# Row gathers, norm terms and row 0 in the passage from the embedding to the attention

## The reference

```python
# embedding: LoRA (rank 16) on a table of 32000 rows, with a norm over the whole table
base = weight[x]
result = base + (lora_A.T[x] @ lora_B.T) * 2.0
direction = weight + lora_A.T @ lora_B.T * 2.0
direction_norm = sqrt(sum(direction * direction, axis=0))          # one number for each of 512 columns
h = result * magnitude * direction_norm
# attention: 16 heads of 32, ternary weights, activations quantized by row
h = h + attn(layernorm(h))
# feed-forward: shared expert, and 2 of 8 routed experts of width 352
h = h + ffn(layernorm(h))
```

## Time and profile before

| what | value |
|---|---|
| median of 3 runs | 1496.45 us (1494.9 to 1499.45) |
| the profiled execution, own time | 1491.15 us |
| its span, first to last instruction | 1489.4 us |
| PE busy | 1387.3 us, 93% |
| DVE busy | 1115.1 us, 75% |
| ACT busy | 876.0 us, 59% |
| POOL busy | 410.3 us, 28% |
| mean granted TensorE clock | 0.983 |

### The profile page before, as it was taken

One profiled execution on the slowest core, in us unless ns is written; L12 is line 12 of the kernel. 1 busy time (PEld: TensorE's weight loads), 2 busy tenths in 40 slices (PEclk: granted clock), 3 DMA queues, 4 the chain that ended last, 5 costly groups with the idle time before them and its releaser, 6 DMA issues.

```text
span 1489.4 us, 37546 instructions
## 1 busy us (share of the span) xinstructions
PE 1387.3 (93%) x14294; PEld 1135.9 (76%) x14294; DVE 1115.1 (75%) x2210; ACT 876.0 (59%) x1506; POOL 410.3 (28%) x503
## 2 busy tenths in 40 slices
PE   6587869999999998999999999999999999999998
PEld 1121137777777776999999999988989889999997
DVE  4477847999989986686558787878778777677776
ACT  4688946777778885333335656666566665433331
POOL 6500054445445432013111211111111110034333
PEclk9899979999999999999999999999999999999999
DMA  9999952322322211121116778777776776434366
GB/s 343 385 384 363 418 154 47 79 65 73 75 64 73 69 58 69 61 103 51 48 30 194 252 264 272 237 257 250 256 270 233 249 255 226 176 129 152 129 211 213
DMA packets 77907, 269.43 MB, mean 181 GB/s; under 512 B 9696, under 2 KB 10336, under 8 KB 71392
## 3 DMA queue, kind: packets, MB, share of 16 engines
q1 hardware_dynamic: 61360, 223.88, 42.1%
q0 software_dynamic: 16432, 44.05, 11.3%
HBM read 224.12 MB, written 43.78 MB: 180 GB/s over the span
## 4 chain that ended last, share of the span: by engine, by line
PE 27%; DVE 12%; issue 9%; ACT 8%; DMA 3%; another core or an unknown queue 0%; DVEq 0%; ACTq 0%; SPq 0%
PE up_ps L536 4%; PE up_ps L537 4%; PE up_ps L538 4%; DVE w_split L1693 4%; ACT w_split L1611 4%; DMA w_stage<-packed 3%; PE down_ps L537 3%; PE down_ps L538 3%; PE down_ps L536 3%; DVE h L1835 2%; ACT h_hi L1634 1%; DVE w_split L1694 1%; PE S L536 1%; PE S L537 1%; PE S L538 1%
## 5 line engine op out<-in xcount | busy, mean ns | idle before, releaser
L536 PE MATMUL up_ps<-xT_hi,w_split 128*128 128x256 f32 x1008 | 289.3, 287 | 12.0 <-DVE h L1854 9.8
L538 PE MATMUL up_ps<-xT_hi,w_split 128*128 128x256 f32 x1008 | 285.7, 283 | 0.0
L537 PE MATMUL up_ps<-xT_lo,w_split 128*128 128x256 f32 x1008 | 285.7, 283 | 0.0
L1634 ACT ACTIVATE h_hi<-h 128x256 fp32r<-128x256 f32 (+1 forms) x192 | 80.3, 418 | 267.0 <-DVE h L1835 203.9
L536 PEld LDWEIGHTS up_ps<-xT_hi,w_split 128*128 128x128 f32 x1008 | 193.4, 192 | 16.3 <-issue 13.7
L537 PEld LDWEIGHTS up_ps<-xT_lo,w_split 128*128 128x128 f32 x1008 | 193.6, 192 | 1.2
L538 PEld LDWEIGHTS up_ps<-xT_hi,w_split 128*128 128x128 f32 x1008 | 193.6, 192 | 0.0
L1579 POOL DMA_INDIRECT xr<-x_rows,slot_tokens x71 | 77.0, 1084 | 422.3 <-PE S L1998 377.8
L1611 ACT ACTIVATE w_split<-w_stage 128x1408 fp32r<-128x1408 f32 (+1 forms) x120 | 165.6, 1410 | 24.7 <-DMA w_stage<-packed 23.0
L536 PE MATMUL down_ps<-w_split,h_hi 128*128 128x512 f32 (+1 forms) x405 | 159.7, 394 | 3.1 <-DVE H L1813 3.1
L538 PE MATMUL down_ps<-w_split,h_lo 128*128 128x512 f32 (+1 forms) x405 | 160.9, 397 | 0.0
(11 more groups left out here) (320 smaller groups left out, 3384.2 us busy)
## 6 DMA issues: line engine op xcount, KB each, us to landing
W<-table SPq DMA_DIRECT2D x48, 1280.0 KB, 9.1
w_stage<-packed SPq DMA_DIRECT2D x80, 704.0 KB
w_stage<-packed SPq DMA_DIRECT2D x40, 768.0 KB, 4.4
slot_rows<-y_rows SPq DMA_DIRECT2D x32, 512.0 KB
xr<-x_turned SPq DMA_DIRECT2D x31, 512.0 KB
x_rows<-x SPq DMA_DIRECT2D x32, 256.0 KB, 2.0
x_turned<-x2T SPq DMA_DIRECT2D x32, 256.0 KB, 3.9
out<-H SPq DMA_DIRECT2D x32, 256.0 KB
```

The source lines that it names most:

```text
L536: pe.matmul(out, a_hi, b_hi, start=first, stop=False)
L537: pe.matmul(out, a_hi, b_lo, start=False, stop=False)
L538: return pe.matmul(out, a_lo, b_hi, start=False, stop=last)
L1634: act.activation(h_hi[odd][0:f, j, :], h[0:f, j, :], ACT.Copy).then_inc(h_hi_done, 1)
```

## The change

In `embed`: `EARLY_ROWS` is 5 instead of 6, and POOL waits for the last tile of the table before it issues them. ACT's copy of `sums_ps` and the tiles `square_sums` and `share` are gone. DVE adds the two tiles of `acc`, adds `product`, and adds `sums_ps` times 1/32; PE sums only that one tile. PE makes products that nobody reads (`keep_busy`): two behind the sum, one behind the spread.

In `attend`: PE begins with six more such products, and its waits for the router's weights move to their first use. DVE multiplies row 0 with `S_bc` in place of POOL, and makes its constants behind row 0's statistics. POOL multiplies rows 1 and 2 late in its step instead of first. DVE takes the statistics of rows 1 and 2 behind the scales of the row before, and `QT` of row 0 behind those. PE makes V of row 0 behind its Q and K.

In `experts`: the down products wait for all three parts of their low weights.

```diff
-EARLY_ROWS = 6
+EARLY_ROWS = 5
...
-            pool.wait_ge(w_in[SLOTS - 1], 16 * TRIPS)
+            arrived, before = tile_in[-1]
+            pool.wait_ge(arrived, before + 16)
             for i in range(EARLY_ROWS):
                 early_row(i)
...
-            act.wait_ge(summed, BY_TILE + (CHUNKS - BY_TILE) * (CHUNK_TILES - len(ADDED_TILES)))
-            act.activation(square_sums[:, :], sums_ps[:, :], ACT.Copy).then_inc(sums_out, 1)
...
+            tiles_added = FOLDED + (CHUNKS - BY_TILE) * len(ADDED_TILES)
+            dve.wait_ge(added, tiles_added)
+            dve.tensor_tensor(acc[:, 0, :], acc[:, 0, :], acc[:, 1, :], ALU.add).then_inc(added, 1)
             dve.wait_ge(crossed, done(CHUNKS - 1))
             dve.scalar_tensor_tensor(out=product[:, :], in0=cross_ps[:, :], scalar=2.0 * LORA_SCALE, in1=b_rep[:, :],
-                                     op0=ALU.mult, op1=ALU.mult).then_inc(terms_made, 1)
+                                     op0=ALU.mult, op1=ALU.mult).then_inc(added, 1)
+            dve.wait_ge(added, tiles_added + 2)
+            dve.tensor_tensor(acc[:, 0, :], acc[:, 0, :], product[:, :], ALU.add).then_inc(added, 1)
+            dve.wait_ge(added, tiles_added + 3)
+            dve.wait_ge(summed, BY_TILE + (CHUNKS - BY_TILE) * (CHUNK_TILES - len(ADDED_TILES)))
+            dve.scalar_tensor_tensor(out=acc[:, 0, :], in0=sums_ps[:, :], scalar=1.0 / DH, in1=acc[:, 0, :],
+                                     op0=ALU.mult, op1=ALU.add).then_inc(terms_made, 1)
...
+            def keep_busy(times):
+                for _ in range(times):
+                    pe.matmul(sums_ps[:, :], ones[:, :], b_rep[:, :], start=True, stop=True)
...
-            pe.wait_ge(added, FOLDED + (CHUNKS - BY_TILE) * len(ADDED_TILES))
-            for i in range(len(ADDED_TILES)):
-                add_up(acc[:, i, :], ones[:, 0:1], False, False)
             pe.wait_ge(terms_made, PRODUCT)
-            add_up(product, ones[:, 0:1], False, False)
-            pe.wait_ge(sums_out, 1)
-            add_up(square_sums, share[:, :], False, True).then_inc(totalled, 1)
+            add_up(acc[:, 0, :], ones[:, 0:1], False, True).then_inc(totalled, 1)
+            keep_busy(2)
...
             mm.then_inc(spread, 1)
+            keep_busy(1)
```

The attention's POOL, DVE and PE, and the experts' PE:

```diff
+            def scale_row(seq):
+                pool.wait_ge(h_in[seq.i % ROW_SLOTS], 16 * (seq.i // ROW_SLOTS + 1))
+                pool.tensor_tensor(row(H, seq.i), row(H, seq.i), S_bc[:, :], ALU.mult).then_inc(rows_scaled, 1)
+                pool.wait_ge(rows_scaled, seq.next)
...
-                if ahead3.yes:
-                    pool.wait_ge(h_in[ahead3.i % ROW_SLOTS], 16 * (ahead3.i // ROW_SLOTS + 1))
...
+                if ahead3.yes and ahead3.i > 2:
+                    scale_row(ahead3)
...
                 if ahead3.yes:
+                    if 0 < ahead3.i <= 2:
+                        scale_row(ahead3)
                     if EARLY_ROWS <= ahead3.i + ROWS_AHEAD < SEQS:
...
+            dve.wait_ge(h_in[0], 16)
+            dve.tensor_tensor(row(H, 0), row(H, 0), S_bc[:, :], ALU.mult).then_inc(rows_scaled, 1)
...
-                if ahead2.yes:
+                if ahead2.yes and ahead2.i not in (1, 2):
+                    row_stats(ahead2)
...
-                if now.yes:
+                if now.yes and now.i > 0:
+                    scaled_queries(now)
+                if ahead2.yes and ahead2.i not in (1, 2):
+                    row_moments(ahead2)
+                    if ahead2.i == 0:
+                        constants()
...
+                if ahead2.yes and ahead2.i in (1, 2):
+                    row_stats(ahead2)
+                    row_moments(ahead2)
+                if now.yes and now.i == 0:
+                    scaled_queries(now)
...
-            pe.wait_ge(w_in, 16)
-            pe.wait_ge(small_made, 3)
+            for _ in range(6):
+                pe.matmul(S[:, 0, :], ones[:, :], S_bc[:, :], start=True, stop=True)
...
-                    for k in range(KT):
-                        mm = pe.matmul(bank[3][:, :], xqT[ahead1.b][:, k, :], wT[2][:, k, :], start=(k == 0), stop=(k == KT - 1))
-                    mm.then_inc(v_done, 1)
+                    if not isinstance(ahead1.i, int) or ahead1.i > 0:
+                        project_values(ahead1)
...
                     project(1, bank[1], xqT[ahead1.b]).then_inc(k_done, 1)
+                    if isinstance(ahead1.i, int) and ahead1.i == 0:
+                        project_values(ahead1)
...
-                pe.wait_ge(w_lo_done[2], w + 1)
+                pe.wait_ge(w_lo_done[2], (w + 1) * LO_STEPS[2])
```

More of the change, by code:

```diff
@@ new lines, in row_stats, with row_moments, scaled_queries @@
+            def row_stats(seq):
+                dve.wait_ge(rows_scaled, seq.next)
+                dve.bn_stats(stats[seq.b][:, :], row(H, seq.i)).then_inc(stats_done, 1)
+            def row_moments(seq):
+                dve.wait_ge(stats_done, seq.next)
+                dve.bn_aggr(moments[seq.b][:, :], stats[seq.b][:, :]).then_inc(moments_done, 1)
+            def scaled_queries(seq):
+                dve.wait_ge(scale_bc_done, seq.next)
+                dve.wait_ge(q_done, seq.next)
+                dve.scalar_tensor_tensor(out=QT[seq.b][:, :, :], in0=bank[0][:, :].rearrange("p (k t) -> p k t", k=KT), scalar=qk_scale[:, 0:1],
+                                         in1=scale_bc[:, :].unsqueeze(1).to_broadcast([P, KT, T]), op0=ALU.mult, op1=ALU.mult).then_inc(QT_done, 1)
@@ L966, in body @@
                     dve.tensor_reduce(neg_logit[:, :], bank[1][:, 0:EXPERTS], X_AXIS, ALU.max, negate=True).then_inc(neg_logit_done, 1)
-                if ahead2.yes:
-                    dve.wait_ge(rows_scaled, ahead2.next)
-                    dve.bn_stats(stats[ahead2.b][:, :], row(H, ahead2.i)).then_inc(stats_done, 1)
+                if ahead2.yes and ahead2.i not in (1, 2):
+                    row_stats(ahead2)
                 if ahead1.yes:
@@ L972, in body @@
                     dve.tensor_reduce(absmax[:, :], y[ahead1.b][:, :], X_AXIS, ALU.max, apply_absolute_value=True).then_inc(absmax_done, 1)
-                if now.yes:
-                    dve.wait_ge(scale_bc_done, now.next)
-                    dve.wait_ge(q_done, now.next)
-                    dve.scalar_tensor_tensor(out=QT[now.b][:, :, :], in0=bank[0][:, :].rearrange("p (k t) -> p k t", k=KT), scalar=qk_scale[:, 0:1],
-                                             in1=scale_bc[:, :].unsqueeze(1).to_broadcast([P, KT, T]), op0=ALU.mult, op1=ALU.mult).then_inc(QT_done, 1)
-                if ahead2.yes:
-                    dve.wait_ge(stats_done, ahead2.next)
-                    dve.bn_aggr(moments[ahead2.b][:, :], stats[ahead2.b][:, :]).then_inc(moments_done, 1)
+                if now.yes and now.i > 0:
[4 more added lines that the diff above has]
+                        constants()
                 if ahead1.yes:
@@ L1054, in project, with project_values @@
                 return mm
+            def project_values(seq):
+                for k in range(KT):
+                    mm = pe.matmul(bank[3][:, :], xqT[seq.b][:, k, :], wT[2][:, k, :], start=(k == 0), stop=(k == KT - 1))
+                mm.then_inc(v_done, 1)
             def first_up_half(j, half):
@@ L1144, in body @@
                         pe.wait_ge(parts_copied, back3.next)
+                    if isinstance(back2.i, int) and back2.i == 0:
+                        pe.wait_ge(w_in, 16)
+                        pe.wait_ge(small_made, 3)
                     for k in range(KT):
```

30 lines of the change are left out of this document (13 added, 17 removed).

## The result

The changed kernel took 1486.81 us (median of 5 runs, 1486.21 to 1490.12), the kernel before beside it 1494.9: a ratio of 0.9952, 95% interval 0.9935 to 0.9969. Two more comparisons of the same two kernels, each with 12 runs of the changed one, gave 0.9976 (0.9959 to 0.9992) and 0.9970 (0.9952 to 0.9989), which is 3.6 and 4.5 us. The forecast size lies among the three. Two things have to be explained: why the size came out so near, though a step of the sum was wrong, and why the time fell out of the range all the same.

What follows compares the result with a forecast made beforehand. A full attention loop, so an earlier begin ends earlier; before it a chain of short waiting instructions. Gains of 2.15 before the attention and 2.75 in row 0 made 4.9, off the median 1496.45: 1491.6, range 1488.0 to 1496.5.

Steps and rivals of the forecast that it cites:

- Step 1: Table's stage: five gathers behind the last table tile cost 0, with 1.7 of slack; at the late bound 0.45.
- Step 2: Norm terms ahead of the spread, on DVE instead of PE: DVE copies the total at 202.4, gain 1.33.
- Step 3: Unread PE products around the spread and at the attention's head hold the clock at 1.00: gain 0.8.
- Rival B: Clock falls anyway, the six products end near 217.3 and delay row 0's transposes: gain 1, 1495.5; chance 0.12.
- Step 4: Row 0's way from the attention's begin to its scores: scores at 218.2 instead of 223.11, 2.75 of it this step's.
- Passing through the loop: Attention loop is full, so the 4.9 gained before it passes through, and the expert stages follow.
- the forecast's signs: What the trace would show if right, among them scores near 218 and later scores 11.17 apart.
- Step 5: Experts: down products wait for three low-weight pieces, the last ending 572.6, first product at 608.54; cost 0, at most 1.27 uncovered.
- A: Attention: row 1's scaling, y and scale_bc slip by 0.6 to 1.2 and delay row 0; gain 3.7, 1492.8; chance 0.15.
- C: Block's end: POOL, held by late gathers, starts the root 0.9 late; gain 4.0, 1492.5; chance 0.08.
- D: Unread products at half clock stand ahead of wanted PE work; scores 2.9 later, 1499.3, slower; chance 0.05.

Runs made afterwards that it cites:

- the third profile: Profile of the changed kernel run unaltered a third time; that comparison with the kernel before gave 0.9970 (0.9952 to 0.9989).
- the late gathers alone: The kernel before with five gathers behind the last table tile and nothing else: 0.9998 (0.9982 to 1.0014) of the kernel before.
- the norm terms alone: The kernel before with only the norm terms moved to DVE, one tile summed on PE: 0.9994 (0.9979 to 1.001) of the kernel before.
- the order alone: The kernel before with only the attention's new order and the down products' wait, without unread products: 0.9985 (0.9968 to 1.0003) of the kernel before.
- the first repetition: The changed kernel run once more unaltered: 0.9976 (0.9959 to 0.9992) of the kernel before, 3.6 us.
- without the third product: The changed kernel without the one unread product behind the spread: 0.9984 (0.9971 to 0.9998) of the kernel before.
- combined: The changed kernel with six early gathers, no third product, statistics of rows 1 and 2 behind K_T: 0.9965 (0.9953 to 0.9977) of before, 1487.25 us.
- early gathers, no third product: The changed kernel with six gathers at slot 5's landing and no unread product behind the spread: 0.9965 (0.9952 to 0.9977) of the kernel before.
- V first: The changed kernel with V of row 0 ahead of its Q and K again; one profiled run, 11.50 us from the attention's begin to the scores.

## Why the prediction was right or wrong

**The direction was right, the range wasn't.** 1486.81 lies 1.2 below its lower end. Three comparisons give 7.2, 3.6 and 4.5 us; the forecast's 4.9 is inside all three intervals. The profiles show 3.6 to 4.1 up to the end of the attention. The step that failed in the range is "so I subtract the gain from the median", with its 2 us of spread. That median of three runs, 1496.45, was high by about 5: later sets of 35, 29, 14 and 23 runs of before have medians of 1491.42, 1490.7, 1492.98 and 1490.21. The sum had been made against the profiled execution, whose own time was 1491.15. Less 4.9 that is 1486.3, half a microsecond from what was measured. I had laid those 5.3 to chance in the one profiled run; they were chance in the three others.

**The size: one step too high, and luck on top.** Forecast for the start of the scores was 4.9 ahead, as 2.15 at the attention's begin and 2.75 in row 0. Measured was 4.0 (3.5 in the third profile): 1.1 at the begin and 2.8 in row 0. So the missing microsecond lies at the block's end alone (step 1). That 4.9 lies amid the three comparisons is luck in part: their scatter is wider than the error of the step.

**Step 1, gathers: wrong.** "Cost 0, with 1.7 of slack" looked for the cost at the root, and there it was nil: POOL was free at 202.47 and the root started 203.26. The working even had the landing, at "about 205", and asked only whether a row's user waits for it. The block's end does. POOL's DRAIN lasts until 1.9 after the last packet, and the attention begins at 10.0 to 10.8 after the last add, where early gathers have 9.42. Cost 0.6 to 1.4 us. That the table gains nothing when the gathers start some 6 us later was right, as the late gathers alone showed.
The fifth of a microsecond that the new adds were to cost a gather isn't shown. In the first profile the gathers beside them took 1.77 and 1.75, and the one before 1.54. But in the third profile the two beside them took 1.53 each, as did the same two with the late gathers alone, where DVE stood still:

```profile
202.71 1.53 POOL L74 DMA_INDIRECT H<-table,rows_i  x1 [0.30 <-issue]
203.40 0.69 DVE L370 TENSOR_TENSOR acc<-acc,product 128x512 f32<-128x512 f32 x1
```

What makes a gather last 1.53 or up to 1.96 is open. The Trainium skill (SBUF — State Buffer, "SBUF: two separate sides") has a VectorE instruction with two SBUF inputs and a GpSimd one that reads SBUF lock each other out for a whole instruction. The gather above stood beside such an add of 0.69 and took no longer than without it, so this trace doesn't show the lock for gathers.

**Step 2, norm terms: right.** Forecast 1.33, measured 1.43 at the totals. Alone on the kernel before it moves the attention's begin by 1.64, 0.2 of that in the spread.

**Step 3, unread products: the clock right, the gain wrong.** The clock held, S_bc came 2.25 sooner (forecast 2.15), the six products took 5.4 (5.2) and were out of the way by 0.4. But the 0.8 of the spread went into the wait for the gathers, and with early gathers too the begin stayed at 9.42, 0.1 ahead of the norm terms alone, whose clock had fallen (9.51): POOL's DRAIN ends at 9.17 whatever S_bc does. All nine products are worth 0.3 us at the scores against the variant without them, whose clock rose 1.9 before its scores; Q, K and V are mostly hidden behind DVE's order. Where the clock rose only behind K, row 0 took 0.85 more (the order alone). Rival B's mechanism exists and its price of row 0's transposes was seen as 1.1, but not in this kernel's profiles; in the one with early gathers the clock fell with the same products, so the program alone doesn't decide it.

**Step 4, row 0: right.** Forecast 11.55 from the attention's begin to the scores, measured 11.50. The queue behind row 1's y and DVE's order were as read; moving QT forward gave 0.8. On Q and K ahead of V the prediction gave no price; it is worth 0. DVE's scaling of row 0, the constants behind its statistics and POOL's later scalings were tested together with the rest of the order only (2.0 with the clock low).

**Passing through the loop: right.** 3.95 at the third step and 4.08 at the end, in the first repetition. From the third step on the steps are 11.2 apart in both kernels, as the forecast's signs had it; the 11.1 of its first paragraph is an average with shorter first steps.

**Step 5, the wait in the down products: not tested by itself.** In the changed kernel's first profile the last low part ends at 568.3 and the first down product is at 604.20, so the cover that the prediction counted on was there.

**Rivals.** A, C and D didn't happen: POOL took 1.27 for rows 1 and 2, the root waited for the total and not for a gather (in the third profile, where the tile came late, with 0.2 to spare), and the six products ended in time.

**What stays open.** POOL's DRAIN takes 4.28 with six early gathers, 4.20 with five late ones whose packets have ended, and 4.04 with three. It starts with the root, so an earlier root should end it sooner, but what its length is made of wasn't varied. And why 5 runs of before came out 4 us higher than most later ones isn't known.

## What to carry to other kernels

A transfer that nobody needs yet is not free near the end of a block: in this kernel the block's end waited for it to land, though its issue was long over. So find for every engine the record that ends its part of the block (here the DRAIN), and compare these ends: what is gained on an engine that isn't the latest is lost there. Put prefetches so early that they land first, or into the next block. Where a gain of an early stage is smaller than the scatter of whole runs, count milestones from an instruction just ahead of the edit: here this told 0.1 us where medians of 12 runs couldn't tell 1.6.

## What the runs showed of the hardware

- The next block starts 0.23 to 0.25 us after the latest DRAIN of POOL, PE and DVE, in 17 profiles. That is 2.11 to 2.15 after the last packet of the gathers, in seven profiles, if that is what comes last; 0.25 after PE's last product, and 0.5 after DVE's last copy, if those do.
- POOL's DRAIN took 4.0 to 4.3 us even when the gathers' packets had ended over 5 us before the begin (eight profiles).
- With the two unread products ahead of the spread the granted clock stayed at 1.00 through the spread in ten profiles and fell to 0.50 at 204.6, 5.7 after the last add, in an eleventh. Behind the spread PE stood idle for 2.8 us once, and the clock fell 0.6 into the products after it (without the third product); after 1.8 idle it fell 0.35 into them in one profile (combined) and held in another (early gathers, no third product); after 2.3 it held (V first).
- The start of one and the same instruction, the last add near 199 us, scatters by 6 us between profiles, up to the end of the stage that streams the table.
